# Gates of a mixture-of-experts kernel turned by VectorE, and its last batch decoded a second time in centred weights

## The reference

```python
x = x + _layernorm(attention(_layernorm(x)))                    # scores/sqrt(128), softmax
e = sigmoid(_layernorm(x) @ W_enc + b_enc)                      # 128 -> 256
cont = e @ W_s2c + b_s2c                                        # 256 -> 64
probs = softmax(cont @ Wr + br)                                 # 8 experts
gate = the two largest probs, divided by their sum, else 0      # (tokens, 8)
h = relu(einsum('tm,emh->eth', cont, W1) + b1)                  # 64 -> 128, 8 experts
y = einsum('eth,ehm->etm', h, W2) + b2                          # 128 -> 64
out = einsum('etm,te->tm', y, gate)
s2 = sigmoid(out @ W_c2s + b_c2s)                               # 64 -> 256
decoded = s2 @ W_dec + b_dec                                    # 256 -> 128
z = (decoded - mean) * rsqrt(var + eps) * ln_g + ln_b
x = x + (z - mean(z)) / sqrt(var(z) + eps)
```

## Time and profile before

| | |
|---|---|
| median of 3 runs | 132.01 us (131.33 to 133.18) |
| the profiled execution: its own time | 131.94 us |
| its span, first to last instruction | 130.1 us |
| mean granted TensorE clock | 0.976 of full |
| busy: PE, DVE, ACT, POOL | 118.0, 92.6, 61.3, 30.5 us |

### The profile page before, as it was taken

How to read it: one execution, slowest core, us unless ns; L and a number is a source line. 1 busy time by engine, 2 the same in 40 slices (tenths; PEclk the granted TensorE clock), 3 DMA queues, 4 the chain that set the end, 5 groups by cost and what they waited for, 6 DMA issues and landing times.

```text
span 130.1 us, 2478 instructions
## 1 busy us (share of the span) xinstructions
PE 118.0 (91%) x813; PEld 79.4 (61%) x813; DVE 92.6 (71%) x392; ACT 61.3 (47%) x177; POOL 30.5 (23%) x61
## 2 busy tenths in 40 slices
PE   6899999999998999999999998999999999998400
PEld 2556686878645887663677983657566556665300
DVE  0858537698989755888246178968949996689792
ACT  1548764665838676104667660056641105705431
POOL 4423503325240213220000222233000043331531
PEclk9999999999999999999999999999999999999955
DMA  3558700000000019800000196000019759620202
GB/s 116 130 127 227 208 30 3 0 0 3 0 5 0 0 48 283 326 0 0 0 0 0 64 324 266 1 0 5 3 47 327 281 154 322 259 81 0 81 0 83
DMA packets 8843, 12.37 MB, mean 95 GB/s; under 512 B 2641, under 2 KB 5470, under 8 KB 8830
## 3 DMA queue, kind: packets, MB, share of 16 engines
q1 hardware_dynamic: 8190, 12.01, 28.5%
q10 hardware_dynamic: 640, 0.20, 0.7%
HBM read 11.09 MB, written 1.11 MB: 94 GB/s over the span
## 4 chain that ended last, share of the span: by engine, by line
PE 58%; DVE 19%; DMA 8%; POOL 4%; ACT 4%; issue 3%; POOLq 1%; SPq 1%; DVEq 0%
PE ps_t L905 9%; PE ps_s L760 7%; PE ps_o L785 6%; PE ps_s L881 5%; DMA gate_all<-gates 5%; PE ps_o L814 4%; POOL rstd L406 4%; PE ps_t L772 3%; DVE stats L1115 3%; PE ps_c L881 3%; PE ps_c L917 2%; PE ps_a L829 2%; DMA x_in<-in_L_attn_x 2%; DVE gated L1224 2%; ACT probs L495 2%
## 5 line engine op out<-in xcount | busy, mean ns | idle before, releaser
L406 POOL TENSOR_TENSOR rstd<-var_eps,minus_half 128x2 f32<-128x2 f32 (+1 forms) x33 | 25.4, 771 | 93.7 <-DVE var_eps L1120 45.8
L785 PEld LDWEIGHTS ps_o<-v,probsT 128*128 128x128 f32 x128 | 15.7, 191 | 3.5 <-ACT probsT L500 2.5
L785 PE MATMUL ps_o<-v,probsT 128*128 128x128 f32 x128 | 17.5, 279 | 0.1
L905 PE MATMUL ps_t<-gated,w 128*64 128x256 f32 x128 | 16.8, 389 | 0.6 <-DVE gated L1224 0.5
L495 ACT ACTIVATE probs<-ps_s,neg_max 128x512 f32<-128x512 f32 x16 | 11.0, 687 | 11.0 <-DVE neg_max L1143 10.4
L760 PE MATMUL ps_s<-xnT,yT 128*128 128x512 f32 x32 | 16.0, 596 | 0.1
L1143 DVE TENSOR_REDUCE neg_max<-ps_s 128x1 f32<-128x512 f32 x16 | 10.9, 689 | 6.0 <-PE ps_s L760 5.9
L905 PEld LDWEIGHTS ps_t<-gated,w 128*64 128x64 f32 x128 | 8.0, 136 | 8.4 <-DVE gated L1224 4.1
L1224 DVE SCALAR_TENSOR_TENSOR gated<-ps_s,b_minus,gate_all 128x512 f32<-128x512 f32 x14 | 9.9, 745 | 3.3 <-PE ps_s L881 1.8
L516 ACT ACTIVATE spikes<-ps_o,bias_half 128x512 f32<-128x512 f32 x6 | 4.1, 688 | 15.1 <-PE ps_o L814 15.1
L500 ACT ACTIVATE probsT<-ps_t 128x512 f32<-128x512 f32 x16 | 9.5, 592 | 2.0 <-PE ps_t L772 1.8
(11 more groups left out here) (184 smaller groups left out, 213.3 us busy)
## 6 DMA issues: line engine op xcount, KB each, us to landing
gate_all<-gates SPq DMA_DIRECT2D x12, 512.0 KB, 6.2
gate_all<-gates SPq DMA_DIRECT2D x8, 256.0 KB, 3.7
x_in<-in_L_attn_x SPq DMA_DIRECT2D x3, 256.0 KB, 3.8
w<-in_L_ffn_W SPq DMA_DIRECT2D x3, 256.0 KB, 4.2
out<-x_out SPq DMA_DIRECT2D x3, 256.0 KB, 2.0
x_in<-in_L_attn_x SPq DMA_DIRECT2D x2, 128.0 KB, 2.7
out<-x_out SPq DMA_DIRECT2D x2, 128.0 KB, 1.8
w_enc<-in_L_ffn_W_enc SPq DMA_DIRECT2D x1, 128.0 KB, 2.8
```

The lines of the kernel that those rows point to most:

```text
L406: nc.gpsimd.tensor_tensor(rstd[part], var_eps[part], minus_half[:, t0:t1], ALU.pow).then_inc(g_rstd[n], 1)
L785: mm = nc.tensor.matmul(attn_out(t), probsT[:, b % 2, t, k], v[:, b % 2, k], start=(k == 0), stop=(k == T - 1))
L905: mm = nc.tensor.matmul(ps_t[h * M:(h + 1) * M, 0:SH], w2[:, e], gated[:, e, h * SH:(h + 1) * SH], start=False, stop=(e == E - 1))
```

## The change

Two edits.

**Gates.** VectorE writes `gate` with the expert ahead of the tile and turns it itself, in 32 x 32 blocks, by one instruction (`nc.vector.transpose`). ScalarE no longer copies anything: it stores the blocks to `gates` in DRAM in pieces of 32 numbers (128 bytes), 128 of them where 8 rows of 2 KB were. `gateT` is then loaded back from `gates` by a DMA of SyncE that stands between the second and the third spreading load. `turn_gates` is gone. `expert_biases` waits for that DMA, and for batches 0, 1 and 2 it stands behind the first experts instead of ahead of them, so `expert_out(b, 0)` opens the sum.

**The last batch's end.** Early on, GpSimd and VectorE make `w_z`, the decoder weights times ln_g with each row's mean taken off, the same of the bias (`b_z`, put as three bf16 rows into `b_z_stack`), and ln_b less its mean (`b_centred`). After decoding the last batch as before (for its variance) TensorE decodes it once more with these weights (`decode_scaled`). VectorE makes z from that PSUM result in one instruction a tile (`z_last`), and z has mean zero. So `dec_scale`, `z_scale`, the centring and the means are gone for this batch. The variance of the first half of z comes from squares on ScalarE (`z_square`, `z_last_var`), that of the second half from `z_stats` as before.

The core of the diff:

```diff
@@ sync
                     sp.wait_ge(v_gated, E * (b - 1))
+                    sp.wait_ge(pe_moe, b - 1)
+                else:
+                    sp.wait_ge(g_zero_rows, 4)
                 for j, (e0, e1) in enumerate(FETCHES):
+                    if j == 2:
+                        sp.dma_start(gateT[0:E, b % 2], gates_dram[b].ap()).then_inc(d_gateT[b % 2], 16)
...
@@ gpsimd, behind inverse_std(LN_X, 3, 0)
+            nc.gpsimd.tensor_tensor(w_scaled[:, :, :], w_dec[:, :, :],
+                                    g_all[:, :].unsqueeze(1).to_broadcast([P, HC, D]), ALU.mult).then_inc(g_scaled, 1)
+            nc.gpsimd.tensor_tensor(b_scaled[:, :], b_dec_sum[:, :], g_all[:, :], ALU.mult).then_inc(g_scaled, 1)
...
@@ gpsimd, behind inverse_std(LN_Z, 0, 0): seven small instructions
+            nc.gpsimd.tensor_copy(b_z_hi[:, :], b_z[:, :]).then_inc(g_bz, 1)
...
@@ scalar
             def gate_out(b):
-                act.wait_ge(pe_gT, b + 1)
...
-                nc.scalar.activation(gateT[0:E, b % 2], gates_bank(b)[0:E], ACT.Identity).then_inc(a_gT, 1)
-                act.wait_ge(a_gT, b + 1)
-                act.dma_start(gates_dram[b].ap(), gateT[0:E, b % 2]).then_inc(d_gate_out[b], 16)
+                act.wait_ge(v_gate_blocks, b + 1)
+                act.dma_start(gates_dram[b].ap().rearrange("e (t j r) -> j (e t) r", t=T, r=32),
+                              gate_blocks[:, b % 2]).then_inc(d_gate_out[b], 16)
...
+            def z_square():
+                act.wait_ge(v_z, T * (B - 1) + TH)
+                for t in range(TH):
+                    nc.scalar.activation(z_squares[:, t], z[:, (B - 1) % 2, t], ACT.Square,
+                                         accum_out=z_square_sum[:, t:t + 1]).then_inc(a_z_square, 1)
@@ tensor
-            def turn_gates(b):
...
             def expert_biases(b):
+                pe.wait_ge(d_gateT[b % 2], 16 * (b // 2 + 1))
...
+            def decode_scaled(h):
...
+                nc.tensor.matmul(bank[:, t0 * P:t1 * P].rearrange("p (t d) -> p t d", d=D), ones_bf[:, :],
+                                 b_z_stack[:, :].unsqueeze(1).to_broadcast([P, t1 - t0, D]), start=True, stop=False)
+                for t in range(t0, t1):
+                    for c in range(HC):
+                        mm = nc.tensor.matmul(bank[:, t * P:(t + 1) * P], spikes2[:, b % 2, c, t * P:(t + 1) * P],
+                                              w_z[:, c], start=False, stop=(c == HC - 1 and t == t1 - 1))
+                mm.then_inc(pe_scaled, 1)
...
                 hidden_pair(b, 1)
-                expert_biases(b)
                 for e in range(4):
                     expert_out(b, e)
+                expert_biases(b)
@@ vector
-                nc.vector.tensor_tensor(gate[:, i], pick1[:, i], pick2[:, i], ALU.add).then_inc(v_gate, 2)
+                nc.vector.tensor_tensor(gate[:, i].rearrange("p e t -> p t e"), pick1[:, i], pick2[:, i],
+                                        ALU.add).then_inc(v_gate, 2)
+                dve.wait_ge(v_gate, count + 9)
+                if b >= 2:
+                    dve.wait_ge(d_gate_out[b - 2], 16)
+                nc.vector.transpose(gate_blocks[:, i], gate[:, i].rearrange("p e t -> p (e t)")).then_inc(v_gate_blocks, 1)
...
+            def z_last(h):
+                b = B - 1
+                dve.wait_ge(g_rstd[LN_DEC], parts_done(LN_DEC, b, h))
+                dve.wait_ge(pe_scaled, h + 1)
+                dve.wait_ge(v_scaled, 3 * (HC + 2))
+                for t in range(*HALVES[h]):
+                    nc.vector.scalar_tensor_tensor(z[:, b % 2, t], scaled_bank(h)[:, t * P:(t + 1) * P], inv(LN_DEC, b, t),
+                                                   b_centred[:, :], ALU.mult, ALU.add).then_inc(v_z, 1)
...
             row_max(3, 1)
+            scaled_weights()
             router_top(1)
...
             dec_var(B - 1, 0)
-            dec_scale(B - 1, 0)
             dec_var(B - 1, 1)
-            z_scale(B - 1, 0)
-            z_stats(B - 1, 0)
-            z_means(B - 1, 0)
-            dec_scale(B - 1, 1)
-            z_scale(B - 1, 1)
+            z_last(0)
+            z_last(1)
+            z_last_var()
             z_stats(B - 1, 1)
-            z_means(B - 1, 1)
             z_add(B - 1, 0)
             z_add(B - 1, 1)
```

More of the change, by code:

```diff
@@ L127, in attention_moe_block @@
         pick2 = sb("pick2", [P, 2, T, E])
-        gate = sb("gate", [P, 2, T, E])
+        gate = sb("gate", [P, 2, E, T])
+        gate_blocks = sb("gate_blocks", [P, 2, E * T])
         gateT = sb("gateT", [P, 2, S])
@@ L243, in attention_moe_block @@
         d_ln = sem("d_ln")
+        d_gateT = [sem(f"d_gateT{i}") for i in range(2)]
         d_gate_out = [sem(f"d_gate_out{b}") for b in range(B)]
@@ L682, in _ @@
                 dec_square(B - 1, h)
-            for h in range(2):
-                z_centre(h)
+            z_square()
         @block.tensor
@@ L843, in route @@
                 mm.then_inc(pe_logit, 1)
-            def turn_gates(b):
-                pe.wait_ge(v_gate, 9 * (b + 1))
-                if b == 1 or b == 2:
-                    pe.wait_ge(a_c2s, HC * b)
-                for t in range(T):
-                    mm = nc.tensor.transpose(gates_bank(b)[0:E, t * P:(t + 1) * P], gate[:, b % 2, t], ident[:, :])
-                mm.then_inc(pe_gT, 1)
             def hidden_pair(b, p):
@@ L883, in hidden_pair, with sum_bank @@
                 mm.then_inc(pe_h, 1)
[L886 to L890 removed]
+            def sum_bank(b):
                 if b + 2 < B:
@@ L897, in expert_biases @@
                     pe.wait_ge(a_moe, b)
+            def expert_biases(b):
+                pe.wait_ge(d_gateT[b % 2], 16 * (b // 2 + 1))
+                if b == 0:
+                    pe.wait_ge(v_b2, 1)
+                if b == B - 1:
+                    sum_bank(b)
                 for h in range(2):
                     nc.tensor.matmul(ps_t[h * M:(h + 1) * M, 0:SH], b2_plus[:, :], gateT[:, b % 2, h * SH:(h + 1) * SH],
-                                     start=True, stop=False)
+                                     start=(b == B - 1), stop=False)
             def expert_out(b, e):
+                first = e == 0 and b < B - 1
+                if first:
+                    sum_bank(b)
+                if b == 0 and e == 0:
+                    pe.wait_ge(d_w2, 32)
                 pe.wait_ge(v_gated, E * b + e + 1)
@@ L905, in expert_out @@
                     mm = nc.tensor.matmul(ps_t[h * M:(h + 1) * M, 0:SH], w2[:, e], gated[:, e, h * SH:(h + 1) * SH],
-                                          start=False, stop=(e == E - 1))
+                                          start=first, stop=(e == E - 1))
                 if e == E - 1:
@@ L1031, in _ @@
                     turn_h(n)
-                if more:
-                    turn_gates(b)
                 scores(m, 3)
-                if not more:
-                    turn_gates(b)
                 attend(m, 1)
@@ L1075, in _ @@
             encode(3, 1)
-            turn_gates(2)
             decode(1, 0)
@@ L1084, in _ @@
             hidden_pair(2, 1)
-            expert_biases(2)
-            turn_gates(3)
             expert_out(2, 0)
@@ L1091, in _ @@
                 expert_out(2, e)
+            expert_biases(2)
             hidden_pair(3, 0)
@@ L1107, in _, with statistics @@
                 decode_part(3, h)
+            for h in range(2):
+                decode_scaled(h)
         @block.vector
         def _(dve):
-            def statistics(n, b, i, source):
+            def statistics(n, b, i, source, elsewhere=0):
                 t0, t1 = parts(n, b)[i]
```

92 lines of the change are left out of this document (66 added, 26 removed).

## The result

The changed kernel takes 132.84 us (median of 16 runs, 132.21 to 136.43); the kernel before took 131.99 us (131.13 to 134.41) beside it. The ratio is 1.008, with a 95% interval from 1.0055 to 1.0106: it is slower by 0.6 to 1.1%, some 1.1 us, where 0.2 us was predicted. That is inside 2%, and inside the range of 131.0 to 133.6. In the execution profiled first, TensorE got its full clock only at 13.5 us instead of 6.2, and all that follows came 3.3 us later, so the rows of after are those of a second one: 133.12 us, span 131.2, 1.18 us above before's 131.94.

What follows compares the result with a forecast made beforehand. TensorE was taken as the bound (58% of the chain), with three waits that matter. +0.62 (through batch 1) + 0.56 - 0.96 = +0.22 us on the profiled 131.94 gave 132.16, and 132.2 for the median; range 131.0 to 133.6.

Steps and rivals of the forecast that it cites:

- Batch 0: Batch 0: turn_gates' removal gives 0.28 us, biases behind the fourth expert cost 0.44; sum +0.16, between 0 and +0.44.
- The early part: free: Set-up of the last batch's weights on VectorE and GpSimd: hidden in waits and idle time, costing nothing.
- Batch 1: Batch 1: later third gates load, then biases at 0.44 us; ends +0.62 late, replacing batch 0's 0.16.
- x: Extra time of the gates' store in 128-byte pieces: taken as 0.5 us, bounds 0 and 1.5.
- Batches 2 and 3, +0.56: Batches 2 and 3: turn_gates -0.2, transpose +0.27, biases +0.44, third load +0.05; bounds 0 and +1.6 us.
- +0.05 for a third load that is late by a little: Batches 2 and 3: a slightly late third spreading load of the gates, costing 0.05 us.
- The end, -0.96: Last batch's end: adding the last half ends at 127.05 instead of 128.01 us; bounds -0.5 and -1.3.
- (1): Gates' store: the pieces land late; 133.1 us at x = 1, 134.1 at x = 1.5; chance 0.22.
- (2): TensorE keeps turn_gates' gain and x is 0: 131.5 us, or 131.0 with batch 2's biases absorbed; chance 0.18.
- (3): The end doesn't shorten, as z_last waits for the second decoding: 133.1 us from 1 us of delay; chance 0.08.
- if the set-up of the weights delays hn or the router: Early part: sign of being wrong, that the weights' set-up, counted as free, delays hn or the router.
- If the store lands in over 2.5 us: Gates' store: sign of being wrong, that it takes over 2.5 us to land.

Runs made afterwards that it cites:

- e7: The gates' edit alone, but with expert_biases ahead of the first experts as in the kernel before: 131.82 us, ratio 0.9982.
- e9: The kernel before with only expert_biases moved behind the experts: 133.07 us, ratio 1.0104.
- e6: The whole change, with GpSimd's ln_g multiplications behind the third batch's inverses and the split of b_z on VectorE: 132.31 us, ratio 1.0004.
- e11: e8 with gateT's load behind the spreading load VectorE waits for (batches 0 to 2) and the biases inside that wait: 130.52 us, ratio 0.9894.
- e3: The end's edit alone on the kernel before, gates unchanged: 131.67 us, ratio 0.9968.
- e8: The whole change with expert_biases early and the set-up moved as in e6: 130.43 us, ratio 0.9863.
- e12: e11, but batch 2 has its biases and gateT's load early again, as in e8: 130.79 us, ratio 0.9933.
- e1: The changed kernel once more, unaltered, beside the kernel before: 133.3 us, ratio 1.0083.

## Why the prediction was right, and where its steps were not

That the two kernels lie within 2% of each other was right, and so was the range. The size was not: +0.22 us predicted for the profiled execution, +1.1 measured, a difference that the measurement could tell from no change. The range had been drawn wide for a late store; what filled it were two costs put at nothing or next to nothing, the set-up and the fourth load. That it held was in part luck. By its steps:

- **Batch 0, +0.16; measured +0.63.** The biases are +0.43 for +0.44 (worked out as 0.47 and entered as 0.44): right, by the same reading (they had stood in TensorE's wait, and now stand behind it); e7 and e9 show it from both sides. `turn_gates` gave 0.36 for 0.28: right in kind. What failed is the step "The early part: free". GpSimd's two multiplications cost 0.56 us, though no instruction waits for their result: they hold up the xn beside them, on which h0's work depends since VectorE turns the gates. I had asked what waits for the set-up, and not what runs beside it.
- **Batch 1, +0.46 on top; measured +0.10.** x, the store's price for pieces, was taken as 0.5 and is 0.48 to 0.53 in batches 0 to 2. (With x = 1 the same steps give +1.12, not +1.06.) The load of experts 2 and 3 landed at 79.89, for 79.84 predicted, but all had moved by 0.62 by then. Against h4 the store is issued 1.11 us earlier, not 0.85, and from its issue to the load's landing it takes 9.01 instead of 8.24 us (+0.77, for +0.93). The load comes 0.34 earlier, and the biases are +0.43. By the same steps the prediction had the load 0.07 us later against h4.
- **Batches 2 and 3, +0.56; measured +1.16** (-0.03, +0.22, +0.97). The transpose is +0.22 for +0.27, the biases +0.43 for +0.44. `turn_gates` gave 0.22 for 0.2 where the set-up is quiet (e6), and 0.03 with GpSimd's seven small operations beside the router, which I had as free. The term "+0.05 for a third load that is late by a little" is the one mis-sized: the load that binds is the fourth, of experts 4 and 5, and it costs 0.53, in the execution profiled first 0.17. In before it landed 0.24 us ahead of where it starts to cost (0.56 for 0.80), which no row that I read said. Its issue isn't late: `gateT`'s place in SyncE's queue puts it 0.26 us back behind the first load (1.57 for 1.31), but all are issued 0.58 us earlier against h11, so it starts 0.32 earlier. It takes longer: 6.58 us from issue to landing for 5.49, over all executions 5.56 to 7.07 where `gateT`'s load is issued ahead of it, and 5.25 to 5.92 with the gates of before. In e11, with `gateT`'s load behind it, it took 5.59. Whether that load is the cause, no run tests by itself. The landing scatters with the gates of before too, from 0.27 to 1.00 us after h11.
- **The end, -0.96; measured -0.80**, and -1.15 in each other kernel with the new end (e3 to e6, e8, e11, e12). The steps were right, `z_last(1)` released by TensorE among them. In the changed kernel VectorE begins `z_last(1)` 0.40 us after the wait in front of it has ended (125.64 to 126.04), in e3 0.05 (124.50 to 124.55). Both profiled executions of the changed kernel have 5.21. Why it pauses there is open.
- **The rivals.** (1), a late store, did not hold as put: x is 0.5, not 1. Nor is it the moving of pieces that costs: from the first packet's start to the last one's end the store took 0.36 us for 0.34. Of the 0.48 to 0.53 us, 0.41 to 0.46 lie ahead of the first packet, in which time the issue on ScalarE's queue is itself 0.24 to 0.54 us longer. The store before has 9 landing events and the new one 5. By the rule of the Trainium skill that the prediction named (DMA: Bandwidth & Descriptors, why a DMA increments its semaphore by 16), 8 and 4 engines; the trace agrees, with one event beside those of the engines. x nearer to 1 was not borne out, but for batch 3, where the store runs beside the spreading loads of batch 2 and took 4.34 us, 1.66 more than before, without a stretch behind it getting longer. (2), faster, needed the waits to absorb the biases. (3) did not hold: the second decoding kept `z_last(1)` waiting for 0.2 us (125.40 to 125.59). Of the signs of being wrong, "if the set-up of the weights delays hn or the router" was the true one. "If the store lands in over 2.5 us" came true in batch 3 and meant nothing, since the store there took 2.69 us in the kernel before.

Summed with the sizes of e1: +0.56 and +0.19 for the set-up, +1.29 for the biases' place in three batches, +0.53 for the fourth load, +0.22 for the transpose, -0.36, -0.22 and -0.34 for the gates' shorter way, -0.80 for the end: +1.07.

## What to carry to other kernels

Work placed in GpSimd's idle time was free here only where nothing critical ran on VectorE beside it: list what the two do at that time before calling it hidden. Work that stands in a wait was free, and behind the instruction that the wait was for it cost its full length, so the same two matmuls (four records) were worth 0 or 0.43 us a batch by their line alone. For a series of loads, ask of each by how much it lands ahead of its use, not only of the one that was waited for before; a small margin, here 0.24 us, is soon used up. And compare two executions of one program before pricing a stretch: here they differed by up to 0.37 us in one.

## What the runs showed of the hardware that was not expected

- GpSimd beside VectorE: `w_scaled` (128x256, 0.74 us) and `b_scaled` (128x128, 0.46) stretch four xn from 1.11 to 1.68 us; a 0.42 us operation on one partition of 128 numbers stretches a 128x32 addition on VectorE from 0.19 to 0.40.
- A store of 16 KB in 128 pieces of 128 bytes took 1.92 to 2.00 us from issue to landing in batches 0 to 2 of e1, in 8 rows of 2 KB 1.44 to 1.47 in before; its issue on ScalarE's queue 0.52 to 1.07 us for 0.27 to 0.54. The packets themselves took as long either way (0.36 and 0.34 us): the pieces cost ahead of the first packet.
- One of 16 parts of a spreading load can land about 1 us behind the other 15 (79.61 after 78.47 in before, 79.16 after 77.81 in e11, 103.23 after 102.30 in e12), and the load counts from then. For experts 2 and 3 of batch 1 it is the rule, 0.67 to 1.50 us in every profiled execution but e9's (0.15): in before 15 parts were there at 78.47, ahead of the 79.27 at which VectorE began to wait. Why is open.
